# A gated cross-attention block on one core: a new head and tail, the weights' preparation spread over batches 0 and 1, and stacked keys with a block's two halves side by side

## What is computed

```python
hs = layernorm(x)                                   # (32, 100, 256)
q, k, v = hs @ Wq.T + bq, ctx @ Wk.T + bk, ctx @ Wv.T + bv     # 16 heads of 16
scores = clip(where(attend, clip(q k / 4, -50, 50), -10000), -50, 50)
delta = (softmax(scores) @ v) @ Wo.T + bo
delta = rs * delta
delta = (delta - mean) / sqrt(var + 1e-5) * ln_gamma + ln_beta
x = x + tanh(g_xattn) * delta
h = silu(bitlinear(layernorm(x), w1)) * bitlinear(layernorm(x), w2)
x = x + tanh(g_ffn) * bitlinear(h, w3)
# bitlinear: activations rounded to 127 steps of their row's maximum,
# weights rounded to -1, 0, 1 times the mean of their magnitudes
```

## Time and profile before

| | us |
|---|---|
| runs shown | 1331.07, 1332.48, 1334.24 |
| median of them | 1332.48 |
| profiled execution, its own time | 1329.38 |
| its span, first to last instruction | 1327.6 |
| TensorE matmul busy | 1282.6 |
| VectorE busy | 1069.2 |
| ScalarE busy | 947.9 |
| GpSimd busy | 394.4 |

### The profile page before, as it was taken

The page is one execution under the profiler, slowest core; times in us unless marked ns, Lnnn a source line. Parts: engine busy times, 40 slices in busy tenths (PEclk is TensorE's granted clock), DMA queues, the critical chain, the costliest instruction groups (busy, mean ns, idle before and its releaser), DMA issues.

```text
span 1327.6 us, 47302 instructions
## 1 busy us (share of the span) xinstructions
PE 1282.6 (97%) x19802; PEld 1177.7 (89%) x19802; DVE 1069.2 (81%) x2085; ACT 947.9 (71%) x1561; POOL 394.4 (30%) x695
## 2 busy tenths in 40 slices
PE   5999999999999999999999999999999999999983
PEld 4988998999999999999999999999999999999972
DVE  5777888779888789886888886888778889778864
ACT  4766777677777767776767776777777877777761
POOL 4322333222333231322331323331233331133310
PEclk9999999999999999999999999999999999999986
DMA  8867777677777777777676768766777776777630
GB/s 238 204 161 180 168 171 183 168 173 182 170 170 184 174 175 174 169 170 197 171 171 168 178 160 203 174 168 160 175 188 176 180 170 163 179 182 175 149 78 11
DMA packets 146187, 225.38 MB, mean 170 GB/s; under 512 B 29674, under 2 KB 139310, under 8 KB 145966
## 3 DMA queue, kind: packets, MB, share of 16 engines
q1 hardware_dynamic: 132312, 202.06, 62.5%
q0 software_dynamic: 12288, 19.69, 6.4%
q10 hardware_dynamic: 1366, 0.53, 0.2%
HBM read 57.27 MB, written 3.28 MB: 46 GB/s over the span
## 4 chain that ended last, share of the span: by engine, by line
PE 89%; SPq 4%; DVE 3%; DMA 2%; issue 1%; ACT 1%; POOL 0%; DVEq 0%; POOLq 0%; ACTq 0%
PE sc L1252 23%; PE pvb L1272 20%; PE cb L1307 19%; PE cb L1293 18%; SPq L331 4%; PE mb L1367 2%; PE mb L1335 2%; PE mb L1345 2%; DMA k_st<-k_lo 1%; PE mb L1382 1%; DVE zt L880 1%; PE mb L1374 1%; PE mb L1328 0%; DMA c_in<-in_ctxT 0%; DVE k_lo L793 0%
## 5 line engine op out<-in xcount | busy, mean ns | idle before, releaser
L572 ACT ACTIVATE e_sb<-sc 121x800 f32<-121x800 f32 (+1 forms) x768 | 644.7, 844 | 187.2 <-PE sc L1252 176.5
L1252 PE MATMUL sc<-q_st,k_st 96*121 96x200 f32 (+1 forms) x3072 | 469.4, 275 | 8.3 <-DMA k_st<-k_lo 5.2
L1252 PEld LDWEIGHTS sc<-q_st,k_st 96*121 96x121 f32 (+1 forms) x3072 | 411.1, 185 | 40.0 <-issue 9.0
L802 DVE TENSOR_SCALAR e_sb<-e_sb,hi_b 121x1600 f32<-121x1600 f32 (+1 forms) x384 | 404.2, 1056 | 12.3 <-ACT e_sb L572 12.1
L1272 PE MATMUL pvb<-e_sb,v_sb 121*32 121x100 f32 x12288 | 286.5, 251 | 0.0
L1272 PEld LDWEIGHTS pvb<-e_sb,v_sb 121*32 121x32 f32 x12288 | 265.2, 110 | 23.5 <-issue 20.4
L793 DVE SCALAR_TENSOR_TENSOR k_lo<-cb,bk_c,k_hi 128x484 fp32r<-128x484 f32 (+1 forms) x192 | 134.5, 701 | 132.8 <-ACT k_hi L584 132.5
L492 POOL DMA_DIRECT2D q_st<-bd_hi x256 | 157.5, 619 | 269.2 <-DVE bd_lo L848 263.8
L1307 PE MATMUL cb<-wv_hi,c_hi 128*121 128x256 f32 (+1 forms) x768 | 221.7, 289 | 2.4 <-DVE k_lo L793 1.3
L1307 PE MATMUL cb<-wv_hi,c_lo 128*121 128x256 f32 (+1 forms) x768 | 215.6, 281 | 0.0
L1307 PE MATMUL cb<-wv_lo,c_hi 128*121 128x256 f32 (+1 forms) x768 | 215.5, 281 | 0.0
(11 more groups left out here) (160 smaller groups left out, 1351.1 us busy)
## 6 DMA issues: line engine op xcount, KB each, us to landing
k_st<-k_hi SPq DMA_DIRECT2D x512, 121.0 KB, 3.0
c_in<-in_ctxT SPq DMA_DIRECT2D x64, 484.0 KB, 3.9
k_st<-k_lo SPq DMA_DIRECT2D x256, 121.0 KB, 3.2
k_st<-k_hi SPq DMA_DIRECT2D x256, 119.0 KB, 3.3
c_in<-in_ctxT SPq DMA_DIRECT2D x32, 476.0 KB, 3.8
k_st<-k_lo SPq DMA_DIRECT2D x128, 119.0 KB, 3.0
q_st<-bd_hi POOLq DMA_DIRECT2D x256, 50.0 KB, 3.3
q_st<-bd_lo POOLq DMA_DIRECT2D x128, 50.0 KB, 3.2
```

Source lines behind the costliest of these rows:

```text
L572: nc.scalar.activation(e_sb[e_slot(b, n)][0:TL[n], k * SW:(k + 1) * SW].rearrange("p (o c) -> p o c", o=2), sc[q % NSC][0:TL[n], :, 0:2 * PW],
L802: V.tensor_scalar(e, e, E_LO, hi_b[b.par][0:TL[n], n:n + 1], ALU.max, ALU.min).then_inc(clip_done, 1)
L1252: last = T_.matmul(sc[q % NSC][0:TL[n], e // 2, (e % 2) * PW:(e % 2 + 1) * PW], k_st[st_slot(b, n // TPC)][:, pr // NQ, pr % NQ, t0:t0 + T ...
```

## The change

- `k_st` and `q_st` are laid out with the group of 32 features ahead of the two halves of the features, so that in blocks 0 and 1 a row's two halves lie side by side.
- The fill of v_sb moves from between GpSimd's first power and first stack to its opening; ScalarE's loads and its first program are in another order (scalars and tanh first, `value_bias` behind the first transposes, `value_weights` behind the query).
- Six of the first stack's twelve transfers are issued by ScalarE (`stack_first`), six of the last one's by GpSimd (`stack_last`), which has `x1_rstd` behind them.
- w1 and w2 are loaded behind the stack of block 1 of batch 0, w3 behind that of block 2, the mask behind context block 2. Their magnitudes are taken in steps 5 and 9 of batch 0 and step 1 of batch 1, their quantisation lies in batch 1, steps 3 to 11.
- The variance plus epsilon moves from GpSimd to VectorE in all three normalisations; the residual scale moves into gamma, so that GpSimd's share is one power.
- In the last batch the values of steps 8 and 9 are multiplied before the last half of the last scores.
- `keep_warm` issues matmuls of a matrix of ones into a free bank: 24 and 5 in the head, 8, 10, 12 and 18 in the tail.

```diff
-        q_st = [sb(f"q_st{i}", [3 * QR, KT, NQ, PW], f32r) for i in range(2)]
+        q_st = [sb(f"q_st{i}", [3 * QR, NQ, KT, PW], f32r) for i in range(2)]
...
-        k_st = [sb(f"k_st{i}", [3 * QR, KT, NQ, CW], f32r) for i in range(NKS)]
+        k_st = [sb(f"k_st{i}", [3 * QR, NQ, KT, CW], f32r) for i in range(NKS)]
...
 # SP
+                if not b.base and b.row == 0:
+                    load_first_weights()
                 if nxt2:
                     sp.wait_ge(dve_x, X_V.after(b, "xn"))
                     load_x(b.plus(2))
...
-                stack_k(b, 2)
+                stack_k(b, 2, last_quads)
+                if not b.base and b.row == 0:
+                    load_third_weights()
...
-                stack_k(whole(0, base), 0)
+                if not base:
+                    load_mask()
+                stack_k(whole(0, base), 0, range(NQ) if base else range(NQ // 2))
...
 # GpSimd
+            nc.gpsimd.memset(v_sb[:, :, :, 1:3, :], 1.0 + 1e-8)
             nc.gpsimd.memset(hq[:, F:FT * P], 0.0)
...
             def delta_rstd(b):
-                pool.wait_ge(dve_post, D_V.after(b, "aggr"))
-                alone()
-                nc.gpsimd.tensor_scalar(d_ve[:, :], dmv[:, 1:2], scal[:, 3:4], EPS, ALU.mult, ALU.add
-                                        ).then_inc(pool_post, 1)
-                pool.wait_ge(pool_post, D_P.after(b, "var"))
-                nc.gpsimd.tensor_tensor(d_rstd[:, :], d_ve[:, :], minus_half[:, :], ALU.pow).then_inc(pool_post, 1)
-                pool.wait_ge(pool_post, D_P.after(b, "rstd"))
-                nc.gpsimd.tensor_tensor(d_r[:, :], d_rstd[:, :], scal[:, 2:3], ALU.mult).then_inc(pool_post, 1)
+                pool.wait_ge(dve_post, D_V.after(b, "var"))
+                nc.gpsimd.tensor_tensor(d_r[:, :], d_ve[:, :], minus_half[:, :], ALU.pow).then_inc(pool_post, 1)
...
+            def stack_last(b):
+                slot, _n = c_slot(b, NCH - 1)
+                pool.wait_ge(k_lo_done, KE.after(b, f"{NCH - 1}{KT - 1}"))
+                alone()
+                pool.wait_ge(sc_ready, SCORE.after(b, STEPS * TPC * (NCH - NKS) - 1))
+                for j in range(NQ // 2, NQ):
+                    for part, src in enumerate((k_hi, k_hi, k_lo)):
+                        nc.gpsimd.dma_start(
+                            k_st[st_slot(b, NCH - 1)][QR * part:QR * (part + 1), j, :, 0:CL[-1]].bitcast(f32),
+                            src[slot][QR * j:QR * (j + 1), :, 0:CL[-1]].bitcast(f32)
+                        ).then_inc(k_stacked_last, 16)
...
                         if gd:
                             delta_rstd(gd)
+                        if not nxt and not b.base:
+                            stack_last(b)
                     if n == 4 and gd:
                         x1_rstd(gd)
...
-                if not base:
-                    nc.gpsimd.memset(v_sb[:, :, :, 1:3, :], 1.0 + 1e-8).then_inc(s_setp, 1)
                 stack_q(whole(0, base))
...
 # ScalarE
+            def stack_first(b):
+                act.wait_ge(k_lo_done, KE.after(b, f"0{KT - 1}"))
+                for j in range(NQ // 2, NQ):
+                    for part, src in enumerate((k_hi, k_hi, k_lo)):
+                        act.dma_start(k_st[0][QR * part:QR * (part + 1), j, :, 0:CL[0]].bitcast(f32),
+                                      src[0][QR * j:QR * (j + 1), :, 0:CL[0]].bitcast(f32)).then_inc(k_stacked[0], 16)
...
+                    if not b.base and (b.row, n) in PREPARED:      # (0, 5), (0, 9), (1, 1)
+                        for i in range(2):
+                            magnitudes(2 * PREPARED.index((b.row, n)) + i)
                     exps(b, n, 1)
...
-                act.wait_ge(s_setv, SETV["bqm11"])
                 x_turned(whole(0, base))
+                if not base:
+                    value_bias()
+                    act.wait_ge(s_setv, SETV["bqm11"])
                 x_query(whole(0, base))
+                if not base:
+                    value_weights()
                 for w in range(NT - (ITEM + 1)):
                     ctx_item(whole(0, base), w)
-                    if w >= 3 and not base:
-                        for i in range(2 * w - 6, min(2 * w - 4, 6)):
-                            magnitudes(i)
+                    if w == 1 and not base:
+                        stack_first(whole(0))
...
 # VectorE
                 dv(V.bn_aggr(dmv[:, :], dstat[:, :]))
+                d_wait(b, "aggr")
+                alone()
+                dv(V.tensor_scalar(d_ve[:, :], dmv[:, 1:2], scal[:, 3:4], EPS, ALU.mult, ALU.add))
...
-                    if not b.base and b.row == 0:
-                        if n == 1:
-                            means()
-                        if n in (2, 3, 4, 6, 7, 8):
...
+                    if not b.base and b.row == 1:
+                        if n in (3, 4, 5, 6, 7, 8):
                             for k in range(KT):
...
-                        if n in (7, 8, 9):
-                            (w3_scaled, w3_low, w3_high)[n - 7]()
+                        if n in (9, 10, 11):
+                            (w3_scaled, w3_low, w3_high)[n - 9]()
...
 # TensorE
+                    if not nxt and n == NT - 1:
+                        for pn in range(NT - VISIT, NT - LAG):
+                            pv(b, pn, 0)
+                            pv(b, pn, 1)
...
+            def keep_warm(bank, count):
+                for _ in range(count):
+                    T_.matmul(bank[:, 0:P], ones[:, :], ones[:, :], start=True, stop=True)
...
+            pe.wait_ge(s_setp, SETP["fill"])
+            keep_warm(cb[1], 24)
             pe.wait_ge(s_setp, SETP["identb"])
             x_turn(b0, None, None)
+            keep_warm(cb[1], 5)
...
-                for n in range(NT - VISIT, NT):
+                for n in range(NT - LAG, NT):
                     pv(e, n, 0)
                     pv(e, n, 1)
                 h_turn(last.plus(-1))
                 down(last.plus(-1))
+                keep_warm(cb[0], 8)
                 delta(last, e)
+                keep_warm(cb[0], 10)
...
+                keep_warm(cb[0], 12)
                 x2_turn(last)
                 for i in range(2):
                     up(last, i, 0, sc[0][:, i, :])
                     up(last, i, 1, sc[1][:, i, :])
+                keep_warm(cb[0], 18)
                 h_turn(last)
                 down(last)
```

133 lines of the change are left out of this document (74 added, 59 removed).

## The result

| | before | changed |
|---|---|---|
| median of the runs | 1333.35 us (1331.07 to 1334.24, 4 runs) | 1319.88 us (1319.38 to 1320.42, 4 runs) |
| profiled execution (span) | 1329.38 us (1327.6) | 1319.38 us (1317.6) |
| mean granted clock in it | 0.987 | 0.996 |
| TensorE / VectorE / GpSimd busy between 85 and 1270 us | 1181.18 / 979.26 / 360.45 | 1182.26 / 999.42 / 339.83 |

The ratio is 0.9901, 95% interval 0.9881 to 0.9921: 13.5 us by the medians, 10.0 by the two profiled executions. The prediction was 1324.2 (1318.0 to 1329.5): 8.25 off the profiled execution of before, and 3.1 on top for the median.

What follows compares the result with a forecast made beforehand. TensorE's own stream bounds the middle, so head and tail can win: head -6.9, batches 0 and 1 +1.4, middle 0, tail -2.75 make -8.25 from 1329.38 us, 1321.1; with 3.1 for the median, 1324.2 (1318.0 to 1329.5).

Steps and rivals of the forecast that it cites:

- rival 2: Whole kernel: merged rows free the stacks, batch 1 costs nothing, clock holds through the last scores; 1319.7 us, chance 0.18.
- (c): Head: 24 filler matmuls before the transposes and 5 behind bring query and first keys to full pace; 1.9 us gained.
- (e): Head: the weights' magnitudes leave ScalarE, so TensorE's waits of 0.92 and 0.41 us go; 1.35 us gained.
- (f): Head: half of the first stack issued on ScalarE's queue, six and six under 4 us; counted 0, up to 0.6 lost.
- The rival by the Trainium skill: Head: a second issuing engine saves sequencer time alone; first scores at 27.2, whole at 1325.6 us, no chance given.
- (g): Head, second block: TensorE's 1.08 us wait for the second stack goes, with w1 and w2 loaded behind it; 1.0 us gained.
- (h): Tail: six of the last stack's issues go to GpSimd, against TensorE's wait of 1.24 us; 0.9 us gained.
- (i): Tail: half of the last 128 value matmuls precede the last scores; 0.85 wait against clip 0.5 later, 0.35 us gained.
- (k): Tail: fillers against the half clock shorten the last product, six transposes and eight matmuls; 1.0 us gained, at most 1.6.
- Rival 1: Tail and batch 1: GpSimd is starved by VectorE, its transfers taking 1.2 us each to issue; 1329.1 us, chance 0.15.
- Rival 3: Head and tail: fillers fail, query and first keys stay at half pace, tail fillers run cold; 1328.1 us, chance 0.08.
- rival 4: Middle: merged rows make a stack late in every block; 1342.2 us with two tenths per issue beyond 0.26, chance 0.04.

Runs made afterwards that it cites:

- e1: The changed kernel without any of its 77 filler matmuls; median 1324.92 us, ratio 0.9939 to the kernel before.
- e6: The changed kernel with the loads, magnitudes and quantising of w1 to w3 back where they were before; median 1321.42 us, ratio 0.9885 to the kernel before.
- e3: The changed kernel with all twelve transfers of the first stack issued by SyncE, none by ScalarE; median 1317.11 us, ratio 0.9887 to the kernel before.
- e7: As e3, and six of the twelve transfers of batch 0's second stack issued by GpSimd; median 1324.00 us, ratio 0.9916 to the kernel before.
- e2: The changed kernel with k_st and q_st laid out as before; median 1323.89 us, ratio 0.9931 to the kernel before.
- e5: The changed kernel as it is, traced and timed again; median 1321.40 us, ratio 0.9885 to the kernel before.
- e9: As e3, with the load of batch 1's second context tile issued behind batch 0's second stack; median 1319.79 us, ratio 0.9893 to the kernel before.
- e4: The changed kernel with all twelve transfers of the last stack issued by SyncE, none by GpSimd; median 1322.77 us, ratio 0.9921 to the kernel before.
- e11: The changed kernel with the last 128 value matmuls in one piece behind the last scores, as before; median 1319.32 us, ratio 0.9886 to the kernel before.
- e8: As e3, with 20 instead of 24 head fillers before the transposes and 2 instead of 5 behind; median 1319.14 us, ratio 0.9875 to the kernel before.
- e10: The changed kernel with the tail's eight fillers spread over four gaps around the last but one product; median 1318.74 us, ratio 0.9877 to the kernel before.

## Why the prediction held, and where its steps did not

**The number and the account.** The number came within its range, nearer to rival 2's than to the forecast's. The account of it did not hold: two of its own signs of being wrong came, first scores after 28 us (29.35) and a middle that changed by more than 2 us (2.5), and the wait of about 4 us at batch 2 stayed away. The signs for single steps did come: the split at 0.66, the twelve key matmuls at 2.69, no wait of 1.24 before the last block, the last product at 0.83. The pair's 10.0 us are 3.96 - 0.29 + 2.52 + 3.81, where the forecast had 6.9 - 1.4 + 0 + 2.75. A head that gave 2.9 less was made up for by batches 0 and 1 (1.1), the middle (2.5) and the tail (1.1). That these errors nearly cancelled is luck.

**The offset of the median** was a step that failed. I took the 3.1 us by which the runs of before lay over their profiled execution as something that the changed kernel has as well, and went from 1321.1 to 1324.2. The median of the changed kernel's four runs lies 0.5 over theirs, and those of the twelve experiments between 1.4 under and 5.5 over. In all runs of the kernel before whose clock is on record, the mean granted clock lies between 0.982 and 0.989, and the time goes with it: 1328.83 us at 0.989, 1338.31 at 0.982. The profiled execution (0.987) was one of its good ones. With the fillers the clock is 0.990 to 0.997, without them (e1) again 0.985 to 0.987. By the medians, all across chips, the fillers are worth 3.5 to 5 us, and 5 to 7 when each kernel is set against the one before on its own chip; by the traces, 1.0 to 1.1 at A (against the changed kernel's two) and 1.3 to 3.8 in the end stretch (nine traces with these fillers, 89.45 to 91.89, against e1's 93.24). That is probably more than the 1.9 + 1.0 of steps c and k, and the size stays open.

**Head, 6.9 forecast, 3.96 measured at A.** (a) and (b) are as forecast: 0.66 for the split, xnT at once. (c) the pace came (query 1.03, twelve matmuls 2.69), but the fillers delay transposes and query by 0.6 each; the first stack begins at 15.65 instead of 19.7, 4.05 for the 4.55 of a to d. (e) 0.9 to 1.0 for 1.35 (e6). **(f) is the step that failed**: counted at nothing, with 0.6 as the worst. Two queues of six issues took 6.6 us, not under 4, the copies came late, the clock fell, and the first scores came at 29.35 instead of 25.8. e3 shows it: without the issues on ScalarE they come at 26.58. The rival by the Trainium skill (DMA: Bandwidth & Descriptors, "Issuing engines are not separate DMA queues") gave 27.2 and was right in kind: e7's second queue ended the issues 3 us earlier and moved the wait by 0.3. What neither the sum nor the rival counted is that the engine which issues loses that time for its own work: ScalarE's copies begin at 22.29, behind its last issue. e3 takes away the fall of the clock together with that wait, and why the clock falls is open. (g) the wait at block 1 is gone only because the first scores are late; when they are early it is 1.39 again (e3). Its "12 x 0.64 + 2.9" left out that the engines are full: my reason "no full 16 engines" was never read from the DMA column, which shows 0.94 for 24 to 44 us in the kernel before.

**Batches 0 and 1, +1.4 forecast.** From A to B the changed kernel takes 38.89, 0.29 more than before, and five more traces of the same program there take 39.04 to 41.71: 1.5 more than before in the mean of the six, and 0.7 to 3.5 more than e6. So the size is about the forecast's, and the place and the cause are not. The wait of about 4 at the start of batch 2 isn't there, and the 1.39 of the earlier trace rows is gone; TensorE's idle time lies between 50 and 68 us instead, where the DMA share is 1.03 to 1.07 from 44 to 64 us. GpSimd's issues, the forecast's cause, got shorter (578 ns); the loads of w1 to w3, which the text costed at nothing, now pass through the engines there and are the likely cause.

**The middle, 0 forecast.** Between B and the last query product the changed kernel is 2.5 shorter in the profiled pair; thirteen traces with the change or parts of it take 1145.4 to 1148.1, the one trace of before 1149.74. From 85 us on TensorE waited 2.9 us for stacks before, 1.39 of it at batch 2, and 0.8 in the changed kernel: 2.1 of the 2.5. Without its waits for stacks this distance is 1145.3 to 1146.6 in the thirteen traces and 1146.9 before, so these waits are most of what varies. Neither the old rows (e2) nor the early preparation (e6) bring it back whole. What removes these waits is left open: the moved additions weren't tried alone, and there is only one trace of the kernel before.

**Tail, -2.75 forecast, -3.81 measured** in the pair, and between 1.7 and 4.2 in the seven other traces with this tail. Of the pair's 3.81, 3.29 lie between the last query product and the last value matmul (60.35 for 63.64), and there the clock decides: it was down from 1279 to 1286 before and held in the changed kernel. Four traces with the changed last batch in which it is down as long (e1, e2, e5, e9) take 62.2 to 62.6, so about 2 of the 3.81 are luck. (h) 0.5 to 0.7 for 0.9 (e4). (i) has the wrong sign: 0.5 to 0.8 lost (e11). The "0.5 later" of the last clip is there (0.64); the wait of 0.85 that was to pay for it isn't: at full clock VectorE reads the sums of e11 right after h, without a wait. (k) was mis-sized. From the last value matmul to the end e1 takes 30.73; the traces e2 to e5 and e9, in which the clock had fallen earlier and holds there, take 28.05 to 28.6, which is 2.1 to 2.7 less, where the term had 1.0. The term had "a few tenths" for the eight gate matmuls, which are 1.16, and nothing for the delta product, 1.05. But in the changed kernel, e6, e7 and e8 the clock falls just ahead of the eight fillers, delta begins 1.2 to 2.1 us behind oT, and the same distance is 29.45 to 31.64, from 1.3 less to 0.9 more than e1: what the fillers bring hangs on where the clock falls.

**Rivals.** Rival 2 is the one whose number came, 1319.7: the wait at batch 2 went, and in the profiled execution the clock held through the last scores. But its way there is only half right: the head gave 3 us less than it assumed, the offset of the median 2.6 more, and the merged rows are not shown to have done any of it (e2). Rival 1 didn't come: the six issues in the tail took 0.53 to 0.94 each beside VectorE's clips, 3.7 together. Rival 3 fell with the head's pace (query 1.03, and 2.00 in e1), though the first eight fillers of the tail do run with the clock down; rival 4 fell with the middle.

## What to carry to other kernels

Before an issue of transfers is moved to an idle queue, read two columns: the DMA share of that stretch (at 1.0 a second queue only ended the issuing earlier, e7) and what stands behind the issues in that engine's own program. Matmuls that fill TensorE's gaps brought the full pace here (query 1.03 for 2.00, gate matmuls 1.37 for 2.53), though the clock still fell once in the last batch or right behind it in all traces but two (e10, e11). Fillers belong into the gaps, sized to them, and not between a ready operand and the product that waits for it: the same eight cost 0.06 us with the clock up (e11) and up to 2.1 with it down (e8). When one trace is set against a median, look at the granted clock of both first; an offset between them isn't a constant of the program.

## What was not expected of the hardware

- Twelve issues on one queue took 8.4 us (e3); six on each of two, side by side, 6.6 in the changed kernel, with single ones up to 1.64 us.
- The clock column reads 1.00 before the first grant that the trace holds: in e1 it says 1.00 for 0 to 16 us, while twelve key matmuls take 4.72 us that take 2.69 at full pace. Durations, not that column, tell the pace in the head.
- In the changed kernel the clock fell at 16.2 although TensorE was busy from 4 to 20 us without a gap; what ran ahead of the fall were the short matmuls of one row (1x4 to 1x512) that set up the rows of gamma, beta and the biases. In all eight traces with six issues on ScalarE's queue the clock falls, at 16.2 to 22.6, and in none of the five without them, so chance is unlikely. But up to 16.2 TensorE runs the same matmuls in e3, where it didn't fall, and no run shows how the issues could bring the fall about.
